# Mamba scan on one Trainium2 core: an earlier copy on ScalarE and a later residual on GpSimd at the seam of two sequences

## The reference

```
proj = x @ W_in.T ;  x_s, z, B_s, C_s, dt = split(proj)
u  = silu(causal_conv(x_s, conv_w) + conv_b)
dt = softplus(dt @ W_dt.T + b_dt) ;  A = -exp(A_log)
h_t = exp(dt_t * A) * h_{t-1} + dt_t * B_t * u_t      # for each of 16 states
y_t = sum over states of h_t * C_t, + u_t * D
out = residual + (y * silu(z)) @ W_out.T
out = layernorm(out) * ln_g + ln_b
```

## Time and profile before

| What | Value |
|---|---|
| median of 3 executions | 1468.59 us |
| lowest, highest | 1464.99, 1473.49 us |
| the profiled execution | 1471.69 us |
| its span, first to last instruction | 1469.8 us |
| mean granted TensorE clock | 0.862 of full speed |
| busy over the span: PE, DVE, ACT, POOL | 76%, 63%, 44%, 38% |

### The profile page before, as it was taken

How to read it: one execution, slowest core, us unless ns; L and a number is a source line. 1 busy time by engine, 2 the same in 40 slices (tenths; PEclk the granted TensorE clock), 3 DMA queues, 4 the chain that set the end, 5 groups by cost and what they waited for, 6 DMA issues and landing times. The chain is left out here.

```text
span 1469.8 us, 24099 instructions
## 1 busy us (share of the span) xinstructions
PE 1112.4 (76%) x6792; PEld 853.5 (58%) x6793; DVE 924.0 (63%) x1890; ACT 650.4 (44%) x1439; POOL 561.7 (38%) x882
## 2 busy tenths in 40 slices
PE   2776774689978688888888888883374799999960
PEld 2555553234448578887778877773243666666640
DVE  2757664711039589999999999994376633333327
ACT  1121221233324587888778887771241033333320
POOL 1000000300012277777877778771000155555540
PEclk9767676789989889999999999996555599999985
DMA  5000000011110200000000000002300011111115
GB/s 166 1 0 0 0 1 0 0 43 39 32 29 0 58 1 1 1 0 0 0 0 0 0 0 0 0 0 87 99 29 22 7 36 36 39 37 37 36 48 181
DMA packets 41603, 39.28 MB, mean 27 GB/s; under 512 B 4042, under 2 KB 37475, under 8 KB 41331
## 3 DMA queue, kind: packets, MB, share of 16 engines
q1 hardware_dynamic: 32466, 21.85, 5.2%
q0 software_dynamic: 4608, 9.45, 2.3%
q10 hardware_dynamic: 4496, 7.60, 1.5%
HBM read 29.92 MB, written 8.96 MB: 26 GB/s over the span
## 5 line engine op out<-in xcount | busy, mean ns | idle before, releaser
L1034 DVE TENSOR_TENSOR_SCAN s_hs<-s_dA,bank 128x1024 f32<-128x1024 f32 x128 | 291.8, 2280 | 9.6 <-PE bank L1385 9.5
L1262 POOL TENSOR_SCALAR s_dbuT<-s_dtuT,s_BT 128x256 f32<-128x256 f32 x512 | 239.9, 492 | 11.0 <-ACT s_dtuT L1117 8.9
L1145 ACT ACTIVATE s_dA<-s_dt,aneg 128x255 f32<-128x255 f32 x512 | 213.6, 498 | 0.6 <-DVE s_hs L1034 0.4
L1835 POOL DMA_INDIRECT x_xg<-hf_rows,x_src x72 | 69.7, 968 | 234.8 <-issue 166.3
L1042 DVE TENSOR_TENSOR s_hc<-s_hs,bank 128x1024 f32<-128x1024 f32 x128 | 156.1, 1220 | 5.3 <-PE bank L1373 0.9
L1385 PE MATMUL bank<-const,s_dbuT 128*128 128x128 f32 x1024 | 139.7, 281 | 26.1 <-POOL s_dbuT L1262 26.1
L1875 PE MATMUL bank<-w,x_xT 128*128 x288 | 127.6, 566 | 16.7 <-ACT x_xT L1917 12.0
L1403 PE MATMUL bank<-const,s_hc 128*128 128x128 f32 x1024 | 138.1, 280 | 2.2 <-DVE s_hc L1042 2.2
L1385 PEld LDWEIGHTS bank<-const,s_dbuT 128*128 128x128 f32 x1024 | 119.8, 145 | 32.8 <-issue 26.4
L1403 PEld LDWEIGHTS bank<-const,s_hc 128*128 128x128 f32 x1024 | 120.8, 145 | 2.4 <-DVE s_hc L1042 2.4
L1913 ACT ACTIVATE x_a<-bank 128x448 f32<-128x448 f32 x72 | 39.1, 543 | 150.7 <-PE bank L1875 139.7
(11 more groups left out here) (298 smaller groups left out, 2239.2 us busy)
## 6 DMA issues: line engine op xcount, KB each, us to landing
w<-in_w SPq DMA_DIRECT2D x16, 256.0 KB, 3.0
o_yr<-y_rows SPq DMA_DIRECT2D x8, 512.0 KB, 3.9
w<-in_w ACTq DMA_DIRECT2D x1, 3584.0 KB, 13.5
x_res<-in_x SPq DMA_DIRECT2D x4, 512.0 KB
gate<-gates_d SPq DMA_DIRECT2D x2, 1024.0 KB, 5.6
s_gate<-gates_d SPq DMA_DIRECT2D x2, 1024.0 KB, 7.8
hf_rows<-r_rows SPq DMA_DIRECT2D x8, 256.0 KB, 2.2
out<-o_o ACTq DMA_DIRECT2D x8, 256.0 KB, 2.4
```

The lines of the kernel that those rows point to most:

```text
L1034: dve.tensor_tensor_scan(flat(hs[:, j % 2]), flat(dA[:, j % RING]), bDbu[j % 2], 0.0, ALU.mult, ALU.add).then_inc(S["scanned"], 1)
L1145: ins = act.activation(dA[:, j % RING, h, n, 1:], dt[:, k, h, 1:], ACT.Exp, scale=m.aneg[:, h, 2 * j + n:2 * j + n + 1])
L1262: ins = pool.tensor_scalar(dbuT[:, j % RING, c, n, :], dtuT[:, k, c, :], BT[:, k, c, 2 * j + n:2 * j + n + 1], 1.0, ALU.mult, ALU.mult)
L1835: pool.indirect_dma_start(xg[k][:], None, m.hf_rows[:, :], bass.IndirectOffsetOnAxis(ap=src[k][:, 0:1], axis=0)).then_inc(S["rows"][k], 16)
```

## The change

Two lines of order are changed, one on ScalarE and one on GpSimd; no instruction is added or removed. On ScalarE at j = 5 the copy to `dtuT` comes ahead of the decays of the next sequence's step 0, where it came behind them. On GpSimd the residual of the sequence before moves from j = 5, where it stood between `times_u` and the inputs of the next sequence's step 0, to j = 6, between the inputs of its steps 0 and 1.

```
--- before.py
+++ after.py
@@ -1148,11 +1148,13 @@
 
             def body(b, k, first, prepares):
                 for j in range(SCAN_J):
+                    if prepares and j == 5:
+                        prepare(j, b + 1, 1 - k)
                     if j + AHEAD < SCAN_J:
                         decays(b, k, j + AHEAD, not (first and j + AHEAD < RING))
                     elif prepares:
                         decays(b + 1, 1 - k, j + AHEAD - SCAN_J, True)
-                    if prepares and j != 2:
+                    if prepares and j not in (2, 5):
                         prepare(j, b + 1, 1 - k)
                     if not first:
                         finish(j, b - 1, 1 - k)
@@ -1267,7 +1269,7 @@
                 for j in range(SCAN_J):
                     if prepares and j == 5:
                         times_u(b + 1, 1 - k)
-                    if not first and j == 5:
+                    if not first and j == 6:
                         residual(b - 1)
                     if j + AHEAD < SCAN_J:
                         inputs(b, k, j + AHEAD, not (first and j + AHEAD < RING))
```

## The result

The changed kernel takes 1481.97 us (median of 6, 1481.12 to 1485.2), the kernel before 1468.57 us beside it (median of 6, 1464.99 to 1473.49). The ratio is 1.0098, with a 95% interval from 1.0075 to 1.0122: slower by about 1%, 13.4 us between the medians (11 to 18 us by the interval). The forecast was 1484 us.

The account below looks back on a forecast made before the run. VectorE, 93% busy in the scan phase, was taken as the bound. Delay 17.8, old clock falls -8.4 and new falls +6 gave +15.4 us, hence a forecast median of 1484 us, range 1475 to 1496.

Parts of the forecast that it names:

- The cover that was lost: GpSimd, sequence changes (seams): residual of 2.64 us, formerly inside the `dtuT` wait, now delays step 1's inputs by 1.4 us.
- TensorE's gaps: TensorE at a seam: idle about 0.35 us before step 0's transposes, 0.75 before C rows, 1.4 before step 1's.
- the delay per seam: VectorE's `yz` comes 1.27 us later at each of 14 sequence changes with a residual, 17.8 us in all.
- The clock: TensorE's drops to 1.2 GHz at seams: five old ones go, -8.4 us; as many new ones cost 6 us.
- the gap of 1.61: TensorE's idle 1.61 us before step 0's transposes: claimed needed, but not enough, for a clock fall, costing 1.67 us each.
- Falls at nearly every seam: Rival: TensorE's clock drops at nearly all 14 seams, +26 to +33 us, 1495 to 1501; chance 0.13.
- The delay near its lower end: Part of the near-cancelling rival: `yz` loses 0.8 us per seam, clock stays up, +3 us, 1472; chance 0.12.
- The third rival: Residual hidden on GpSimd, the five falls go and seams win 0.33 us each: -13 us, 1455.6; chance 0.05.

Follow-up runs that it names:

- the shorter residual: Changed kernel with the residual's second operation covering only 16 of 128 columns, so the output lacks part of the second gate row; ratio to before 1.0023.
- The filled kernel: Changed kernel in which TensorE writes the C rows of step 0 four times over while waiting for step 1's inputs; ratio to before 1.0054.
- the residual alone: Kernel before with only GpSimd's residual moved between the inputs of steps 0 and 1, the copy staying behind the decays; ratio to before 1.0298.
- copy alone: Kernel before with only ScalarE's copy to `dtuT` put ahead of the decays, the residual staying at j = 5; ratio to before 0.9942.
- residual in two parts: Changed kernel with the residual's first two operations at j = 5 and its addition to `x_res` at j = 7; ratio to before 0.9944.

## Why the prediction was right

**The cover that was lost.** The step that decides is that the residual filled GpSimd's wait for `dtuT`, and that it would stand between the inputs of steps 0 and 1 instead. The wait came out at 1.70 (forecast 1.66), the residual between the two at 2.64 (2.64). The kernel with the residual at j = 7 shows that this place alone makes the loss; the shorter residual shows its size.

**TensorE's gaps.** 0.39 ahead of step 0 (0.35), 0.80 (0.75) ahead of the C rows, and 1.21 ahead of step 1 where I had 1.4. TensorE began 0.08 after the last input was complete (638.74 + 1.82 = 640.56, to 640.64), not 0.14, and the C rows came some 0.1 later behind the product. So the delay per seam was 1.17 and not 1.27: 16.4 us and not 17.8. At every second seam the two gaps are 0.7 and 1.3 instead, with the same sum and the same delay.

**The clock.** Five falls went and five came. I had forecast as many as before at 1.2 each, 6 us; they cost 0.66 to 1.64 and 5.2 in all. That the number is the same was a guess, and luck: the prediction's own reasoning, that a seam with more idle time is hit more often than before, is not borne out between these two kernels (a gap of 1.61 and two of together 2.0 us, five falls in each). The reading that the gap of 1.61 "is needed" for a fall was wrong too, since the new falls come without one. The filled kernel bears out only that the falls are a term of their own, which the idle stretch makes. The sum is +13.2 us in the scan phase against +15.4; of the 2.2 between them 1.4 are the delay and 0.8 the falls.

**Rivals.** Falls at nearly every seam did not come here, but they do in the kernel with the residual alone, where TensorE has a gap of 1.62 and further ones behind it: 13 of 14. The delay near its lower end did not come either; the cost of the shorter residual shows what it would have been, a kernel within 0.3% of before. The third rival, in which only the first half acts, was priced at -13 us. The kernels that come near its gain (copy alone, residual at j = 7, residual in two parts) have -12 us between the same fifteen rows (418.30 where before has 430.24, for the copy alone: 549.14 to 967.44), and 8 to 10 us by their ratios. The condition that I gave for it, a residual of 2.0 us or less, is met by none of them: they don't shorten the residual but move it to where nothing waits, and that I had not weighed.

**Where I was wrong.** The largest miss was in the expectation for the copy alone: I took the falls as something that might stay at a gap of 1.3 us. What stays open is why five seams fall at a gap of 1.61 and the nine others don't, why none does at 1.41, and why the changed kernel has five again. The count of falls is known for one execution of each kernel; that it is much the same in the others is borne out only by the ratios, which rest on several executions of each.

## What to carry to other kernels

Before moving work out of the way of a critical input, look at what it fills there: work that lies in a wait is free, and behind the wait it is paid for as far as nothing else covers it. Of the residual's 2.64 us, `yz` lost 2.4 where the inputs were not early and 1.17 where they were. If it must move, move it past every input that the bound engine needs soon; one step later made the difference between +1% and -0.7%. And when TensorE waits at regular places, compare equal seams with each other: where some have matmuls of twice the length, a shorter gap, even one filled with repeated matmuls, can be worth more than the wait itself.

## What the runs showed of the hardware

In a kernel whose TensorE is 85% busy over the phase, a single gap of 1.61 us let the granted clock fall at five of 14 seams, each time at a cost of 1.67 us; in kernels with a single gap of 0.97 to 1.41 us it fell at none. Two gaps of 0.80 and 1.21 us with 0.38 us of matmuls between them: five of 14 again, and none once the same matmuls, repeated, filled part of the second gap. Writing the same two bf16 matmuls (128x256) twice instead of once at that gap, 0.2 us of useless work, made the whole kernel 0.7% faster (0.9934, 0.9911 to 0.9956).
